# Splitting the maxima, exponentials and transposes of a pair of attention heads into one head at a time

## The reference, cut to what matters

```python
def _L3_gnn_ref(h, W, adj):                     # h: 64 graphs x 128 nodes x 128
    qkv = (h @ W).reshape(Bn, Nn, 3, H, HEAD_DIM).transpose(2, 0, 3, 1, 4)   # H = 4, HEAD_DIM = 32
    q, k, v = qkv[0], qkv[1], qkv[2]
    mask = jnp.where(adj == 0, -jnp.inf, 0.0)
    scores = jnp.einsum('bhid,bhjd->bhij', q, k) / np.sqrt(HEAD_DIM) + mask
    attn = jax.nn.softmax(scores, axis=-1)
    out = jnp.einsum('bhij,bhjd->bhid', attn, v)
    return out.transpose(0, 2, 1, 3).reshape(Bn, Nn, OUT_DIM)
...
x = _layernorm(x + _L3_gnn_ref(x, L3_gnn_W, adj), axis=-1)
```

## Time and profile before

| what | value |
|---|---|
| runs: median (lowest to highest of 3) | 1474.07 us (1472.52 to 1478.42) |
| the profiled execution: span from first to last instruction | 1472.2 us |
| DVE busy | 1125.0 us, 76% |
| PE busy | 1049.8 us, 71% |
| ACT busy | 803.6 us, 55% |
| POOL busy | 173.0 us, 12% |
| mean granted PE clock | 0.895 |

### The profile page before, as it was taken

One profiled execution on the slowest core, in us unless ns is written; L12 is line 12 of the kernel. 1 busy time (PEld: TensorE's weight loads), 2 busy tenths in 40 slices (PEclk: granted clock), 3 DMA queues, 4 the chain that ended last, 5 costly groups with the idle time before them and its releaser, 6 DMA issues.

```text
span 1472.2 us, 24898 instructions
## 1 busy us (share of the span) xinstructions
PE 1049.8 (71%) x6161; PEld 862.0 (59%) x6161; DVE 1125.0 (76%) x5634; ACT 803.6 (55%) x2921; POOL 173.0 (12%) x464
## 2 busy tenths in 40 slices
PE   5777777777655600006998779988789978899875
PEld 4666666666544500005797566976668966679754
DVE  6888888888799889994457785576865578845687
ACT  3555555555322200003677866767767778677786
POOL 2111111111200000001011110111020120201111
PEclk9999999999986555557999999999899989999998
DMA  0000000000123400004000011000030000100001
GB/s 2 1 1 1 1 1 1 1 1 1 37 54 101 115 1 1 0 1 115 1 1 1 2 32 57 1 2 1 1 88 1 2 1 1 30 1 1 1 1 29
DMA packets 45246, 25.51 MB, mean 17 GB/s; under 512 B 1921, under 2 KB 44066, under 8 KB 45090
## 3 DMA queue, kind: packets, MB, share of 16 engines
q1 hardware_dynamic: 45090, 23.81, 5.8%
HBM read 15.42 MB, written 8.39 MB: 16 GB/s over the span
## 4 chain that ended last, share of the span: by engine, by line
PE 31%; DVE 11%; ACT 8%; issue 3%; POOL 1%; DMA 0%; DVEq 0%; POOLq 0%; ACTq 0%; SPq 0%
PE P L1101 11%; PE P L1109 6%; PE P L1049 6%; PE P L1054 2%; ACT x L1203 2%; ACT S L1271 2%; DVE stats L1310 2%; DVE S L1382 1%; DVE top L1387 1%; PE P L1163 1%; DVE t L1400 1%; PE P L1118 1%; PE P L1147 1%; POOL t L1037 1%; ACT t L1251 1%
## 5 line engine op out<-in xcount | busy, mean ns | idle before, releaser
L193 PE MATMUL productP<-M,ident_tail 128*128 128x127 f32 (+63 forms) x254 | 87.3, 441 | 71.2 <-DVE M L313 71.2
L1101 PE MATMUL P<-t,WihT 128*128 128x128 f32 (+1 forms) x832 | 119.4, 290 | 10.9 <-POOL t L1037 10.9
L1109 PE MATMUL P<-step_h,WhhT 128*128 128x128 f32 (+2 forms) x768 | 123.4, 304 | 0.0
L193 PEld LDWEIGHTS productP<-M,ident_tail 128*128 128x128 f32 x254 | 63.6, 311 | 95.0 <-DVE M L313 95.0
L1101 PEld LDWEIGHTS P<-t,WihT 128*128 128x128 f32 x832 | 109.9, 191 | 14.5 <-POOL t L1037 13.7
L1223 ACT ACTIVATE gate_i<-P,half_bias 128x128 f32<-128x128 f32 (+3 forms) x160 | 69.2, 433 | 88.9 <-PE P L1109 65.0
L1030 POOL TENSOR_TENSOR rstd<-variance,minus_half 128x4 f32<-128x4 f32 x64 | 64.5, 1008 | 430.8 <-DVE variance L1320 430.8
L1109 PEld LDWEIGHTS P<-step_h,WhhT 128*128 128x128 f32 x768 | 108.9, 191 | 4.5 <-DVE step_h L1353 0.7
L464 PE MATMUL sumP<-ident_tail,Yb 128*128 128x128 f32 x1 | 0.5, 473 | 153.2 <-DVE Yb L627 153.2
L190 PE MATMUL tailP<-ident_tail 128*128 128x128 f32 (+63 forms) x254 | 87.7, 443 | 19.9 <-DVE ident_tail L297 8.8
L1340 DVE SCALAR_TENSOR_TENSOR gate_i<-gate_i,gate_g 128x128 f32<-128x128 f32 (+2 forms) x96 | 36.1, 376 | 83.7 <-ACT gate_g L1223 83.7
(11 more groups left out here) (326 smaller groups left out, 3222.5 us busy)
## 6 DMA issues: line engine op xcount, KB each, us to landing
x_here<-x SPq DMA_DIRECT2D x16, 256.0 KB, 3.1
feature_products<-made SPq DMA_DIRECT2D x16, 256.0 KB, 2.4
xin<-x SPq DMA_DIRECT2D x16, 256.0 KB, 2.9
xw<-feature_products SPq DMA_DIRECT2D x16, 256.0 KB, 3.2
out<-y SPq DMA_DIRECT2D x16, 256.0 KB, 2.3
W<-L_gnn_W SPq DMA_DIRECT2D x3, 64.0 KB
Wqkv<-L_gnn_W SPq DMA_DIRECT2D x1, 192.0 KB
Wg<-L_gnn_Wg SPq DMA_DIRECT2D x2, 64.0 KB
```

Source lines behind the costliest of these rows:

```text
L193: pe.matmul(productP[:, remaining], tails, M[:, remaining], start=True, stop=True).then_inc(product_ready, 1)
L1101: last = pe.matmul(place, c["WihT"][:, p - 1, gate * H:(gate + 1) * H], sources(s, p, t), start=bank not in fresh, stop=not t, skip_group_ ...
L1109: last = pe.matmul(gate_place(s, p, t, gate), c["WhhT"][:, p - 1, gate * H:(gate + 1) * H], step_h[s][:, 0:G * windows(p)], start=False, s ...
```

## The change

The triple of a pair becomes two triples of one head: mask, maximum over 128 x 512 (128 x 4 out), negation, first all of head 0 and then all of head 1, each with semaphores of its own (`masked_0`, `tops_0`, `tops_ready_0` and the same with `_1`). ACT waits for `tops_ready_0` before the four exponentials of head 0 and for `tops_ready_1` before those of head 1, and raises `probs_ready_0` and `probs_ready_1`. PE waits for the first before it turns head 0 and for the second before it turns head 1. DVE's reciprocal waits for `probs_ready_1`. The data, the matmuls, the exponentials and all copies stay the same, and so does the order of the stages; no DMA is touched.

```diff
-        return on, on_step, on_later, on_norm, on_pair, on_windows
+        def on_half(name, r, h, s, trip):
+            what = [("softmax" if name == "probs_ready" else "scores", n) for n in range(HEADS // PAIR)]
+            engine.wait_ge(S_(f"{name}_{h}"), trip * (len(what) * SLOTS) + rank(what, r, s))
+
+        return on, on_step, on_later, on_norm, on_pair, on_windows, on_half
...
                 elif name[0] == "probs_turned":
-                    on_pair("probs_ready", name[1], s, trip)
+                    on_half("probs_ready", name[1], 0, s, trip)
                     turn(P[s][0], lambda b: S[s][:, 0, b, :]).then_inc(S_("probs_turned_a"), 1)
+                    on_half("probs_ready", name[1], 1, s, trip)
                     turn(P[s][1], lambda b: S[s][:, 1, b, :]).then_inc(S_("probs_turned_b"), 1)
...
                 elif name[0] == "softmax":
-                    on_pair("tops_ready", name[1], s, trip)
                     for h in range(PAIR):
+                        on_half("tops_ready", name[1], h, s, trip)
                         for b in range(G):
                             k = h * G + b
                             last = A_.activation(S[s][:, h, b, :], S[s][:, h, b, :], ACT.Exp, bias=ntop[s][:, k:k + 1],
                                                  accum_out=total[s][:, k:k + 1])
-                    last.then_inc(S_("probs_ready"), 1)
+                        last.then_inc(S_(f"probs_ready_{h}"), 1)
...
                     for h in range(PAIR):
-                        last = V.scalar_tensor_tensor(S[s][:, h], P[s][h][:].rearrange("n (g m) -> n g m", g=G),
-                                                      float(HEAD) ** -0.5, c["mask"][:, None, :].to_broadcast([N, G, N]),
-                                                      ALU.mult, ALU.add)
-                    signal(last, "masked", s)
-                    on_pair("masked", r, s, trip)
-                    signal(V.reduce_max(top[s][:], S[s][:].rearrange("n h g m -> n (h g) m"), AX_X), "tops", s)
-                    on_pair("tops", r, s, trip)
-                    signal(V.tensor_scalar(ntop[s][:], top[s][:], -1.0, None, ALU.mult), "tops_ready", s)
+                        tops = slice(h * G, (h + 1) * G)
+                        V.scalar_tensor_tensor(S[s][:, h], P[s][h][:].rearrange("n (g m) -> n g m", g=G),
+                                               float(HEAD) ** -0.5, c["mask"][:, None, :].to_broadcast([N, G, N]),
+                                               ALU.mult, ALU.add).then_inc(S_(f"masked_{h}"), 1)
+                        on_half("masked", r, h, s, trip)
+                        V.reduce_max(top[s][:, tops], S[s][:, h], AX_X).then_inc(S_(f"tops_{h}"), 1)
+                        on_half("tops", r, h, s, trip)
+                        V.tensor_scalar(ntop[s][:, tops], top[s][:, tops], -1.0, None,
+                                        ALU.mult).then_inc(S_(f"tops_ready_{h}"), 1)
                 elif name[0] == "probs_turned":
                     r = name[1]
-                    on_pair("probs_ready", r, s, trip)
+                    on_half("probs_ready", r, PAIR - 1, s, trip)
                     signal(V.reciprocal(head_share[s][:, r, :], total[s][:]), "head_share", s)
```

## The result

The changed kernel takes 1479.47 us (median of 15 runs, 1477.08 to 1481.86), the kernel before, run beside it, 1473.89 us (15 runs, 1472.52 to 1479.30). The ratio is 1.0026, 95% interval 1.0015 to 1.0037: slower by about 4 us (2.2 to 5.5), clear of noise, but less than the 0.5% (7.4 us) that the prediction called about no change. The forecast was 1480.3. The runs of the kernel before lie in two groups, near 1473 and near 1478 to 1479, and its profiled one (1474.07) is one of the quicker; what sets them apart is open.

A forecast was written before the change was run, and what follows sets the result against it. The prediction took DVE to bound the heads' part: four uncovered triples of 0.39 us make 1.56 us a trip, 6.2 over four trips, so 1474.07 + 6.2 = 1480.3 us. Range 1474 to 1486 us.

The forecast's parts named there:

- What bounds it: Heads' part of each trip: DVE's lost time reaches the trip's end; exponentials never wait for DVE's maxima.
- D: Rival, heads' part: ACT sets the pace, so five further waits go, some 16 us faster, 1458 us; chance 0.06.
- The growth of a triple: DVE's mask, maximum and negation, split by heads, take 3.04 us instead of 2.65, 0.39 us more.
- A: Rival, DVE's triples: waits within DVE cost nothing, growth 0.23 us, 3.7 us in all, 1477.8 us; chance 0.15.
- Which four stay: Of a trip's eight DVE triples, T1 to T8, growth of T4, T5, T7, T8 stays uncovered: 1.56 us a trip.
- rival B: Rival, PE's burst: longer idle gap keeps its clock at half for 6.80 us, 2.7 us more, 1483.0 us; chance 0.17.
- ACT: Copy of turned head 0: up to 24.8 us of waiting go, becoming some 2 us a trip before exponentials.
- Rival C: DVE's halves: new waits bring register work, a half starts 0.28 us late, 10.7 us more, 1484.8 us; chance 0.06.

The follow-up runs named there:

- e8: The changed kernel with DVE's same six instructions reordered: both masks, both maxima, both negations; 1474.91 us, ratio to the kernel before 0.9986.
- e1: Against the changed kernel, DVE's half triples alone; exponentials wait once for both maxima, PE for all eight exponentials; 1479.16 us, ratio to the kernel before 1.0013.
- e6: The changed kernel with four added matmuls of 128x512 filling PE's gap before the burst; 1475.32 us, ratio to the kernel before 0.9991.
- e5: The kernel before with three added matmuls of 128x512 filling PE's gap before the burst; 1469.19 us, ratio to the kernel before 0.9952.
- e7: e2 with three added matmuls of 128x512 filling PE's gap before the burst; 1469.20 us, ratio to the kernel before 0.9949.
- e2: Against the changed kernel, DVE's triple as before; exponentials wait once but signal each head, PE turns by heads; 1478.24 us, ratio to the kernel before 1.0002.

## Why the prediction was right, point by point

*What bounds it.* Right. DVE carries the part, its loss reaches the end of the trip, and the exponentials wait for no maximum. D fell: no trip was shorter.

*The growth of a triple.* 0.39 us, as forecast, but its parts were wrong. I counted 0.23 for the second maximum and negation and 0.16 for waits and lost overlap. By e8 it is about the other way round: I estimate two more waits for the instruction in front at 2 x 0.115 = 0.23, and the two instructions at the other 0.16 (e8's 2.58 less a triple of before without its two waits, 2.65 - 0.23). Such a wait costs more than the idle of 0.03 that a row shows: what is lost is the overlap with the next instruction, 0.72 us from start to start instead of 0.60, for the maxima as for the masks. The sum held because it was read from a whole half of the same shapes in the third layer and not from the parts. A, by which the waits cost nothing, fell with it. The Trainium skill (VectorE: DVE Perf Modes, "The DRAIN you can't avoid") has it that a semaphore after each instruction costs nothing extra; for waits on the instruction in front this does not hold here, since e8 and the change have the same instructions and semaphores and differ by 0.46 us a triple.

*Which four stay.* I said T4, T5, T7 and T8. In e1, with DVE's halves alone and the clock of the kernel before, the first trip shows three: W is 1.16 us later, three times 0.39, for T5, T7 and T8. T6's growth goes into the wait before T7, as forecast. T4's does not stay in the loop trips: it goes into the 0.40 us that passed behind the negation before T5, 0.28 of them idle. I had read these as register work that moves along; but the register piece is still in its place and T5's mask follows at once, so that reading was wrong, and what the idle is stays open. The written-out last trip has no such idle, and the change lost most there, 2.02 us.

The transposes by heads then let T4 start 0.30 sooner, since its scores stand behind them (I had allowed 0.1 for this, in the lower bound alone), and bring the long stretch at half clock; both together make 35.84 us of e1's 35.66 in the first trip. So it is in part luck that the mean of 1.44 us a trip came near the 1.56 forecast: one of the four triples was not lost in the loop trips, and a longer stretch that the sum left to rival B put part of it back.

At full clock (e6 against e5, first trip) it is four triples again, but another four: the distance grows from -0.28 at T5 to +0.10 at T6, +0.49 at T7, +0.88 at T8 and +1.26 at W, so T5, T6, T7 and T8 stay. T6 is not covered there, since its cover was PE's slow burst, which e5 removes. Four times 0.39 less the 0.30 at T4 is 1.26; the last trip has 1.55, the mean of all four is 1.33.

*ACT.* Wrong in size and place: not "up to 24.8 us gone" but 34.1, and no new idle at the exponentials. The copies that found their transposes done are offset by 2.69 and 1.52 us for transposes that stand in PE's queue behind scores and `mixed`, which wait for DVE. The final effect that I drew from it, nothing for the trip, held in the whole change (36.01 us against 35.82 of e1, which lacks ACT's and PE's halves); but e7 shows that at full clock the transposes by heads are worth 0.42 us a trip, not nothing.

*Rival B.* What it describes happened, gap 4.05 us, 6.80 us at half clock, T6 waiting 1.51, in all four trips. Its price of 0.91 us a trip did not: T7 gets about half of it back (T6 to T7 5.15 us instead of 5.59), the second trip of the kernel before, which has the long stretch, ends 0.62 later than its first, and e5 shows that the kernel before pays for its own slow burst nearly as much as the change. Of its reason one half holds. The length of the gap does not decide: e8 has one of 3.05 us, shorter than before's 3.14, with the long stretch in all four trips, e1 one of 3.56 with the short one in three. But where PE turns by heads (the change, e2, e8) it falls idle 16.2 us behind T1 and the stretch was long in all twelve trips; where it turns by pairs (before, e1) it falls idle at 17.0, and it was long in two of eight. Why in these two stays open; filling the gap ended both.

*Rival C* did not occur: no half starts late behind register work (841.71 to 841.80 above).

The term that carried the sum, DVE's longer triples, was right in kind and was the largest; the sum was 6.2 us, and the heads' parts differ by 5.3 at full clock, by 5.8 as profiled, of which e1 has 5.0.

## What to carry to other kernels

Before splitting a step so that its consumer can start sooner, look whether that consumer ever waits for it: the exponentials waited 0.0 us for the maxima, and only the split behind them (transposes by heads) had 0.42 us a trip to give. If an engine near its limit must do the two halves, put independent instructions between each and the one that waits for it: the same six instructions took 3.04 or 2.58 us by their order alone. And when an engine that is not the bound idles just before a burst on the path, look at its clock in the burst, in the kernel before as well.

## What the runs showed of the hardware

A DVE instruction that waits for the one just in front costs 0.115 us more in the mean than one that does not (four in 0.46 us), and a second maximum of 128x512 next to a first adds almost nothing (1.27 for both against 1.22 for one of 1024). PE's granted clock, at 0.50 for 3.4 or 6.8 us around the burst, stayed at 1.00 there when the idle 3.14 us before it were filled with 2.74 us of matmuls whose results nobody reads: 1.15 us a trip were won by added work. What went with the long stretch was not the gap's length but its start, 0.8 us sooner. A matmul of 128x512 in fp32 ran as two pieces, one every 0.44 us (5.32 / 12).
